# Carrying boxed probabilities in natural key order: eight half transfers a group, and no second copy of the values

## The reference

```
q, k, v = x Wq^T + bq, x Wk^T + bk, x Wv^T + bv          # 256 wide, 8 heads of 32
scores  = (q k^T) * 32**-0.5 * (adj + adj)               # per graph and head, 256 x 256
attn    = softmax(scores)                                 # over the keys
ctx     = attn v                                          # sum over the 256 keys
y       = x + (ctx Wo^T + bo)
out     = (y - mean(y)) / sqrt(var(y) + 1e-5)             # over the 256 channels
```

## Time and profile before

| what | us |
|---|---|
| timed runs, median of 3 | 414.3 |
| the profiled execution, its own time | 411.37 |
| the profiled execution, its span | 409.4 |
| TensorE busy, of the span | 382.1 |
| VectorE busy, of the span | 370.4 |
| ScalarE busy, of the span | 359.0 |
| GpSimd busy, of the span | 273.0 |

### The profile page before, as it was taken

How to read it: one execution, slowest core, us unless ns; L and a number is a source line. 1 busy time by engine, 2 the same in 40 slices (tenths; PEclk the granted TensorE clock), 3 DMA queues, 4 the chain that set the end, 5 groups by cost and what they waited for, 6 DMA issues and landing times.

```text
span 409.4 us, 12272 instructions
## 1 busy us (share of the span) xinstructions
PE 382.1 (93%) x3628; PEld 294.2 (72%) x3628; DVE 370.4 (90%) x1335; ACT 359.0 (88%) x1224; POOL 273.0 (67%) x507
## 2 busy tenths in 40 slices
PE   8997999999899979999999989799999999988692
PEld 7764777777678857778777767677777778866471
DVE  3997799999989969999999998969999999999765
ACT  4699899999899959999999979959999999999750
POOL 3252557786777756787777866747677877556665
PEclk9998999999999989999999999989999999999988
DMA  8478877988988888999888889889998988887803
GB/s 268 136 199 236 218 217 200 257 210 255 257 231 241 223 212 264 272 259 251 242 215 239 254 244 254 217 230 239 263 246 259 233 219 232 236 216 215 229 27 103
DMA packets 65428, 92.30 MB, mean 225 GB/s; under 512 B 8529, under 2 KB 48722, under 8 KB 65362
## 3 DMA queue, kind: packets, MB, share of 16 engines
q1 hardware_dynamic: 47426, 66.35, 63.4%
q10 hardware_dynamic: 17936, 25.17, 18.3%
HBM read 26.22 MB, written 8.39 MB: 85 GB/s over the span
## 4 chain that ended last, share of the span: by engine, by line
PE 62%; SPq 12%; ACT 8%; DVE 7%; DMA 5%; issue 4%; POOL 2%; DVEq 0%; ACTq 0%; POOLq 0%
PE proj_bank L334 16%; PE row_bank L265 11%; PE ctx_bank L405 11%; SPq L209 7%; PE out_bank L422 7%; PE out_bank L352 7%; ACT probs L729 6%; PE turn_bank L282 5%; DMA carried<-boxes 4%; SPq L218 3%; DVE boxes L538 3%; PE turn_bank L367 2%; DVE probs L525 2%; PE turn_bank L454 1%; DVE context L553 1%
## 5 line engine op out<-in xcount | busy, mean ns | idle before, releaser
L729 ACT ACTIVATE probs<-probs,low_top 128x256 f32<-128x256 f32 x512 | 254.8, 509 | 4.4 <-POOL low_top L937 4.4
L525 DVE CUSTOM_DVE_ANT_0 probs<-row_bank,adj_rows 128x256 f32<-128x256 f32 x512 | 181.5, 420 | 13.5 <-PE row_bank L265 10.7
L538 DVE STREAM_TRANSPOSE boxes<-probs 128x1536 f32<-128x1536 f32 x62 | 109.6, 1767 | 0.0
L729 ACT ACTIVATION_READ_ACCUMULATOR probs<-probs,low_top 128x1 f32 x512 | 102.6, 200 | 0.0
L334 PE MATMUL proj_bank<-xt_parts,w_parts 128*128 128x512 f32 x360 | 99.9, 413 | 0.0
L334 PEld LDWEIGHTS proj_bank<-xt_parts,w_parts 128*128 128x128 f32 x360 | 63.2, 189 | 33.7 <-issue 22.5
L937 POOL TENSOR_SCALAR low_top<-top 128x4 f32<-128x4 f32 x128 | 25.5, 199 | 88.7 <-issue 51.4
L265 PE MATMUL row_bank<-kq 32*128 32x256 f32 x1024 | 73.8, 402 | 0.2 <-DVE top L525 0.2
L405 PE MATMUL ctx_bank<-carried,v_boxed 128*32 128x256 f32 x744 | 63.5, 402 | 8.1 <-DMA carried<-boxes 7.9
L405 PEld LDWEIGHTS ctx_bank<-carried,v_boxed 128*32 128x32 f32 x744 | 29.8, 113 | 35.7 <-issue 21.7
L265 PEld LDWEIGHTS row_bank<-kq 32*128 32x128 f32 x1024 | 46.5, 184 | 12.5 <-issue 6.2
(11 more groups left out here) (86 smaller groups left out, 448.0 us busy)
## 6 DMA issues: line engine op xcount, KB each, us to landing
carried<-boxes SPq DMA_DIRECT2D x248, 192.0 KB, 4.3
xt<-in_x_t SPq DMA_DIRECT2D x32, 256.0 KB, 4.5
adj_rows<-in_adj ACTq DMA_DIRECT2D x32, 256.0 KB, 4.9
xr<-in_x ACTq DMA_DIRECT2D x32, 256.0 KB, 4.2
v_boxed<-v SPq DMA_DIRECT2D x124, 64.0 KB, 3.1
out<-result ACTq DMA_DIRECT2D x31, 256.0 KB, 5.1
w_whole<-in_wk ACTq DMA_DIRECT2D x2, 128.0 KB, 3.6
w_whole<-in_wq SPq DMA_DIRECT2D x1, 256.0 KB, 4.3
```

The lines of the kernel that those rows point to most:

```text
L525: last = nc.vector.tensor_tensor_reduce(probs[:, h % RING, t * S:(t + 1) * S], row_bank[j][:, t * S:(t + 1) * S], adj_rows[:, (g // 2) % 2 ...
L538: nc.vector.transpose(boxes[:, n % BOXES].rearrange("p a h (f q) -> p (h f) a q", q=D), probs[:, first:first + BOXED, :].rearrange("p h (f ...
L729: last = nc.scalar.activation(tile, tile, ACT.Exp, bias=low_top[:, g % 2, J * c + j, t:t + 1], accum_out=sums[:, g % 2, t, j * T + c:j * T ...
```

## The change

- `box`: the blocks are cut otherwise. The 128 keys of a tile are two halves `e` of 64, and block `a` of a half takes every other key of it: 64e + 2k + a. The instruction reads with a step of two numbers where it read neighbours; it writes what it wrote, as many numbers.
- `carry_boxes`: a carry DMA takes the two blocks of one half `e` from one band `i` and writes 64 partitions. Key 64e + 2k + a lands on partition 64e + 2k + a, its own number. It takes eight DMAs a group in place of four, 96 KB each; `carried_in` counts 128 a group.
- `carry_v`, `v_boxed` and `v_in` go. `weigh_v` reads `v` in all 32 matmuls of a graph and waits no more for `v_in`.

```diff
+                for e in range(2):
+                    for i in range(J):
+                        sp.dma_start(carried[P // 2 * e:P // 2 * (e + 1), g % 2, c, i].rearrange("p h f -> p (h f)"),
+                                     boxes[D * i:D * (i + 1), n % BOXES, J // 2 * e:J // 2 * (e + 1)].rearrange("p j h f -> p j (h f)")
+                                     ).then_inc(carried_in[n % 4], 16)
-                for i in range(J):
-                    sp.dma_start(carried[:, g % 2, c, i].rearrange("p h f -> p (h f)"),
-                                 boxes[D * i:D * (i + 1), n % BOXES].rearrange("p j h f -> p j (h f)")
-                                 ).then_inc(carried_in[n % 4], 16)
-
-            def carry_v(n):
-
-                sp.wait_ge(v_ready, n + 1)
-                wait(sp, ctx_made, n - 3)
-                for j in range(J):
-                    sp.dma_start(v_boxed[j::J, (n // 2) % 2, n % 2].rearrange("p t e -> p (t e)"),
-                                 v[D * j:D * (j + 1), (n // 2) % 2, n % 2].rearrange("p t e -> p (t e)")
-                                 ).then_inc(v_in[n % 4], 16)
...
-            carry_v(0)
...
-                if 0 <= g + 1 < LAST:
-                    carry_v(g + 1)
...
-                if g < LAST:
-                    pe.wait_ge(v_in[g % 4], 64 * (g // 4 + 1))
...
-                        pe.wait_ge(carried_in[n % 4], 64 * (n // 4 + 1))
+                        pe.wait_ge(carried_in[n % 4], 128 * (n // 4 + 1))
...
-                                                    values[:, (g // 2) % 2, g % 2, t, o * D:(o + 1) * D], tile, start=(t == 0),
+                                                    v[:, (g // 2) % 2, g % 2, t, o * D:(o + 1) * D], tile, start=(t == 0),
...
-                    dve.wait_ge(carried_in[(n - BOXES) % 4], 64 * ((n - BOXES) // 4 + 1))
+                    dve.wait_ge(carried_in[(n - BOXES) % 4], 128 * ((n - BOXES) // 4 + 1))
...
-                nc.vector.transpose(boxes[:, n % BOXES].rearrange("p a h (f q) -> p (h f) a q", q=D),
-                                    probs[:, first:first + BOXED, :].rearrange("p h (f a k) -> p (h f) a k", a=J, k=D)
+                nc.vector.transpose(boxes[:, n % BOXES].rearrange("p (e a) h (f q) -> p (h f) e a q", q=D, e=2),
+                                    probs[:, first:first + BOXED, :].rearrange("p h (f e k a) -> p (h f) e a k", e=2, a=J // 2, k=D)
```

More of the change, by code:

```diff
@@ L64, in build @@
         v = sb("v", [P, 2, 2, T, E])
-        v_boxed = sb("v_boxed", [P, 2, 2, T, E])
         top = sb("top", [P, 2, H, T])
@@ L103, in build @@
         stored = [sem(f"stored{n}") for n in range(2)]
-        x_in, adj_in, v_in, carried_in = (
-            [sem(f"{name}{n}") for n in range(4)] for name in ("x_in", "adj_in", "v_in", "carried_in"))
+        x_in, adj_in, carried_in = (
+            [sem(f"{name}{n}") for n in range(4)] for name in ("x_in", "adj_in", "carried_in"))
         xt_in = [[sem(f"xt_in{n}_{t}") for t in range(T)] for n in range(2)]
@@ L394, in weigh_v @@
                             if g == LAST:
-                                values = v
                                 tile = last_tile(c, j)[:, t * S:(t + 1) * S].rearrange("p (u i q) -> p u i q", u=T, i=J)
                             elif j < BOXED:
-                                values = v_boxed
                                 tile = carried[:, g % 2, c, :, j, :].rearrange("p i (u t q) -> p t u i q", u=T, t=T)[:, t]
                             else:
-                                values = v
                                 tile = turned_probs[:, (2 * g + c) % 4, t * S:(t + 1) * S]
```

## The result

The changed kernel takes 409.96 us in the median of 20 timed runs (404.71 to 413.19), the kernel before 416.1 us on the same chips (411.18 to 424.46). The ratio is 0.9876, 95% interval 0.9845 to 0.9908: faster by 1.2%. It leaves out of both kernels the runs that lie over 1.5% above the kernel's fastest (the slow ones), so it isn't the quotient of the two medians, 0.985. The forecast was 404 of 414.3 us, a ratio of 0.975, or 2.5% faster. The direction is right and the time lies in the range, but the gain is half of what was forecast. The profiled execution took 408.42 us with a span of 406.6, 2.8 us less than the one of before; the timed runs differ by more, since the profiled execution of before lies at the low end of its 20 runs.

What follows compares the result with a forecast made beforehand. TensorE was taken to bound the kernel, SyncE's issuing second. The profiled 411.4 us less 11.5 for late carries gave 399.9; 2.9 for the timed median made 402.8, and 1.2 for remaining late groups 404 us, range 400 to 427.

Steps and rivals of the forecast that it cites:

- What bounds: Kernel before: TensorE at 11.41 us a graph, SyncE's issuing second, just under it; late carries lose 11.5 us.
- A free issue: SyncE's queue: 0.63 us from one issue to the next, so 17 issues take 10.9 us a graph with gaps.
- Holding back: SyncE's issues held until transfers ahead drain: 0.5 us a graph taken, making 11.4, level with TensorE.
- deciding point: SyncE's pace of 11.87 us a graph, 0.70 us an issue, at which the time equals the 414.3 us of before.
- middle case: Rival "nothing changes": holding back of 0.7 to 1.1 us a graph eats the gain, 412 to 416 us; chance 0.13.
- The formula: Time if SyncE needs r us a graph: 402.8 + 29 x (r - 11.41) - 2, for 29 graphs and 2 us slack.
- signs named for being right: `weigh_v` every 11.4 us, few TensorE carry waits, carry issues near 0.6, SyncE awaiting `box`, DMA share near 0.81, `box` 1.77.
- The rule on halves: Carry DMAs: the skill says not to split a transfer into two partition halves, since both serialize on the same engines.
- the first rival: SyncE takes TensorE's place: slower drains or dearer issues make 17 exceed 11.41 us, 427 us at 0.72 an issue; chance 0.24.
- 218 GB/s for halves: Carry DMAs: 64 partitions reach half of 16 ports, so half of 436 GB/s would be the most halves get.
- The step of two in `box`: VectorE's `box` read: taken to cost nothing; the rival, 0.75 us more a `box`, gives 445 us, chance 0.07.
- Latency: Carries from `box` to `weigh_v`: 10.5 us available, the last of eight lands after 8.1, slack 2.4.

Runs made afterwards that it cites:

- x4: The kernel before without `carry_v`, its four carries of 192 KB a group kept whole (output wrong): ratio 0.9645 to the kernel before, span 398.0 us.
- x1: The changed kernel with each carry taking one head of three from the fifth group on, same issues (output wrong): ratio 0.9736 to the kernel before, span 400.6 us.
- x3: The changed kernel with a group's eight carries reordered so that neighbours read and write other halves: ratio 0.986 to the kernel before, span 408.6 us.
- x5: The changed kernel with one more issue a graph on SyncE's queue, a 1 KB copy nothing reads: ratio 1.0216 to the kernel before, span 422.1 us.
- x6: The changed kernel with three more 1 KB copies a graph on SyncE's queue: ratio 1.0741 to the kernel before, span 445.9 us.
- x8: x1 with 256 more waits a graph on TensorE, all on a semaphore met from the start; the waits doubled the time.

## Why the prediction was half right

- *What bounds*: right for the kernel before. SyncE's queue was the second bound, and the late carries cost 11.5 us. x4 gives back 11.4. Of these 11.5 us, the 3.6 that no wait names fit TensorE's clock: in that stretch the trace grants 0.5 of the clock, the lower level, twice for 3.41 us (from 146.5 and from 266.0 us, each at the end of a wait of 2.5 us), which costs at most 3.4 us.
- *A free issue, 10.9 us a graph*: right. The median is 602 ns and the gap 43, and 17 x 0.645 = 10.97.
- *Holding back, "I take 0.5 us"*: this is the step that failed. It measured 1.0 us a graph (0.9 when the few issues under 0.60 us are set against it). The reasoning asked only which bytes stand ahead of an issue, and that part went as reasoned: the median of all carries fell to the free price. But in x1, with a third of the bytes, 0.75 us of it stay. They sit in about one long issue a graph, each beside a 16 KB packet of instructions. The trace of before held such packets and issues near them, unread, hidden among many others that were late for the transfers ahead.
- So the pace is 10.97 + 0.9 = 11.87 us by these terms, and measured 11.88, in place of "11.4: level with TensorE, hidden". With nothing to spare, the 0.47 us a graph above TensorE's 11.41 bring late carries back: TensorE waited for them 9 times, 8.2 us. The sum had taken off the whole 11.5 us and put back 1.2. By the prediction's own measure 11.88 is 0.70 us an issue, its deciding point. What came is its middle case ("r near 11.85"), which it priced at 412 to 416 and gave 0.13.
- *The price of that pace*: too high. The formula gives 399.9 + 29 x 0.47 - 2 = 411.5 for the profiled execution, which took 408.4. It let 29 graphs pay; the first carry that TensorE waited for came at 108.6 us. It also took the profiled execution as 2.9 us below the median of before, where the 20 runs put it at 4.7; the changed kernel's lies only 1.5 below its own.
- *The range, and "faster"*: both held, in part by luck. The mechanism behind them, TensorE bound throughout, did not come; a pace slower than forecast and a price for it that was too high set each other off in part. Of the signs named for being right, the median of the carry issues and `box` came. TensorE's 11.4 us throughout and SyncE's wait for `box` in each graph didn't, and the DMA share is 0.86 from 60 to 350 us, where about 0.81 was forecast (0.88 before, over the same stretch).
- *The rule on halves* (DMA: Bandwidth & Descriptors, Rules for kernel authors, of the Trainium skill): measured, the split costs 2.4% here, so its advice holds. Its reason, that halves share the engines and serialize, is not what decides: x3 changes how they collide and not the time, x5 adds an issue without bytes and costs 15.5 us. The eight issues more a graph use up the queue's slack; x1 shows that with fewer bytes the same issues cost only 2.6 us over x4. The rule bears on the first rival of the prediction's list (it says the second). Its 218 GB/s for halves was not put to the test: the 220 GB/s that passed hold ScalarE's transfers too.
- *The step of two in `box`*: 1768 ns against 1767, nothing, as taken. The Trainium skill's rule that the prediction used (two hits for each 16-byte line; SBUF — State Buffer, Specifications) agrees.
- *Latency*: right in kind. Halves land 0.9 us sooner than wholes.

## What to carry to other kernels

Count the DMA issues of each queue per step, price each at its duration plus gap, and hold the sum against the step of the engine that bounds, with room to spare: here 10.9 of 11.4 us was not enough. An issue costs the queue its time even when it moves 1 KB; before a transfer is split in two, look for one that can go to another queue. And read the longest issues one by one before a median is put into a sum, for part of them may have a cause that the change leaves alone.

## What the runs showed of the hardware

- The cost of an issue on SyncE's queue goes by what was issued before: 590 ns for 1 KB behind a carry, 454 to 459 behind another such copy, 430 for 256 KB behind three of these (x5, x6).
- An issue behind whole carries of 192 KB takes longer from the third on: 575, 613, 761, 987 ns by place in the kernel before. Behind halves of 96 KB it doesn't: 601 to 604 ns in the changed kernel.
- Beside a 16 KB packet of TensorE's instructions, an issue on SyncE's queue often takes 1.1 to 1.9 us in place of 0.60: all 22 issues above 1.1 us of x1 stood beside one. Which resource the two share was not tried.
- 128 instructions in a row that only wait on a met semaphore keep TensorE idle for 12.9 us, 0.10 us each (x8). They cost more than that: while TensorE so stands idle, the granted clock falls to 0.5, its lower level, for 13.65 us or more in each graph. The first six matmuls behind them took 2.90 us, the next such six, at the full clock, 1.65:

```profile
112.11 2.90 PE L322 MATMUL proj_bank<-xt_parts,w_parts 128*128 128x512 f32 x6 [12.89 <-issue]
...
121.53 1.65 PE L322 MATMUL proj_bank<-xt_parts,w_parts 128*128 128x512 f32 x6
```
